# All loops written out, and matmuls without a reader, in a two-layer kernel of linear attention and patch-FFT convolution

## The reference

```python
x = x + L0(_gn(x), ...)   # attention without softmax, 6 heads of 64
x = x + L1(_gn(x), ...)   # 1x1 conv, filter in 8x8 patches, 3x3 depthwise conv, gate, 1x1 conv

# L0
q = elu(rope(Wq x + bq) * scale) + 1;  k = elu(rope(Wk x + bk)) + 1;  v = Wv x + bv
kv = einsum('bhnd,bhne->bhde', k, v)
normalizer = einsum('bhnd,bhd->bhn', q, k.sum(axis=2))[..., None]
out = einsum('bhnd,bhde->bhne', q, kv) / (normalizer + 1e-06)
return conv1x1(out, Wfc, bfc)

# L1
t = einsum('bchw,oc->bohw', x, w_in)
t = irfft2(rfft2(patches of 8x8 of t) * fft_filter)
t = depthwise 3x3 conv of t with w_dw, 'SAME'
g = gelu(t[:, :192]) * t[:, 192:]
return einsum('bchw,oc->bohw', g, w_out)
```

## Time and profile before

| | us |
|---|---|
| median of 3 runs | 3960.15 |
| lowest, highest | 3959.14, 3964.23 |
| the profiled execution | 3959.47 |
| its span | 3957.6 |
| its mean granted clock, of full | 0.944 |

### The profile page before, as it was taken

One profiled execution on the slowest core, in us unless ns is written; L12 is line 12 of the kernel. 1 busy time (PEld: TensorE's weight loads), 2 busy tenths in 40 slices (PEclk: granted clock), 3 DMA queues, 4 the chain that ended last, 5 costly groups with the idle time before them and its releaser, 6 DMA issues.

```text
span 3957.6 us, 61233 instructions
## 1 busy us (share of the span) xinstructions
PE 3490.4 (88%) x17808; PEld 3021.8 (76%) x17808; DVE 3178.0 (80%) x4879; ACT 1629.6 (41%) x2781; POOL 1795.7 (45%) x1114
## 2 busy tenths in 40 slices
PE   5988989889898898988989889897889979899798
PEld 4976779767796677966779677896768957699676
DVE  7976979769797697976879768897688976888777
ACT  2423634246342463425633255332553316533164
POOL 2543535435354353553435534454344544444443
PEclk9998989999998999999989899898999989999899
DMA  5113322133212332123321233213332133221322
GB/s 201 64 56 136 119 77 69 64 120 120 89 56 72 121 119 81 57 87 120 112 76 61 88 112 112 89 48 103 109 107 81 48 114 109 96 81 56 128 88 104
DMA packets 186274, 371.18 MB, mean 94 GB/s; under 512 B 7947, under 2 KB 9011, under 8 KB 185779
## 3 DMA queue, kind: packets, MB, share of 16 engines
q1 hardware_dynamic: 186034, 368.26, 27.2%
HBM read 267.56 MB, written 100.66 MB: 93 GB/s over the span
## 4 chain that ended last, share of the span: by engine, by line
issue 33%; PE 30%; POOL 18%; DVE 14%; ACT 3%; DMA 1%; POOLq 1%; DVEq 1%; SPq 0%; ACTq 0%
POOL t L445 9%; POOL x_lo L438 6%; PE bank L1234 5%; PE bank L1200 3%; DVE bank L942 3%; PE bank L1075 3%; PE bank L1076 3%; PE bank L1080 3%; POOL qn L482 3%; PE bank L1207 3%; DVE nrm L850 2%; DVE qt_lo L865 2%; PE bank L1154 2%; DVE xr L878 2%; DVE bn_x L911 2%
## 5 line engine op out<-in xcount | busy, mean ns | idle before, releaser
L445 POOL TENSOR_TENSOR t<-t 128x768 f32<-128x768 f32 x256 | 535.4, 2092 | 726.4 <-DVE t L786 726.4
L1076 PE MATMUL bank<-w_lo,x_hi 128*128 128x384 f32 x2322 | 792.7, 341 | 34.1 <-issue 34.1
L1075 PE MATMUL bank<-w_hi,x_hi 128*128 128x384 f32 x2322 | 789.7, 340 | 4.0 <-ACT x_hi L537 4.0
L438 POOL TENSOR_TENSOR x_lo<-xa,x_hi 128x512 fp32r<-128x512 f32 x363 | 495.9, 1382 | 592.0 <-ACT x_hi L537 592.0
L942 DVE SCALAR_TENSOR_TENSOR bank<-big,wdw,bank 128x512 f32<-128x512 f32 x960 | 685.7, 750 | 94.5 <-PE bank L1234 91.3
L506 POOL TENSOR_TENSOR prod<-prod 128x512 f32<-128x512 f32 x320 | 409.1, 1278 | 489.1 <-ACT prod L629 479.0
L542 ACT ACTIVATE t<-t 128x768 f32<-128x768 f32 x256 | 217.1, 848 | 929.1 <-POOL t L445 929.1
L1080 PE MATMUL bank<-w_hi,x_lo 128*128 128x384 f32 x2322 | 542.3, 342 | 0.5 <-POOL x_lo L438 0.5
L796 DVE SCALAR_TENSOR_TENSOR kt<-t 128x384 f32<-128x384 f32 x256 | 533.6, 2084 | 0.0
L1076 PEld LDWEIGHTS bank<-w_lo,x_hi 128*128 128x128 f32 x2322 | 441.4, 190 | 36.3 <-issue 36.3
L1075 PEld LDWEIGHTS bank<-w_hi,x_hi 128*128 128x128 f32 x2322 | 442.3, 190 | 5.1 <-ACT x_hi L537 4.4
(11 more groups left out here) (127 smaller groups left out, 6800.2 us busy)
## 6 DMA issues: line engine op xcount, KB each, us to landing
xr<-x SPq DMA_DIRECT2D x128, 768.0 KB, 4.7
xa<-x SPq DMA_DIRECT2D x66, 768.0 KB, 6.0
x_scratch<-xr SPq DMA_DIRECT2D x64, 768.0 KB, 3.5
xa<-x_scratch SPq DMA_DIRECT2D x64, 768.0 KB, 5.9
xr<-x_scratch SPq DMA_DIRECT2D x64, 768.0 KB, 4.8
out<-xr SPq DMA_DIRECT2D x64, 768.0 KB, 3.5
big<-x SPq DMA_DIRECT2D x8, 768.0 KB, 10.3
w_raw<-wqkv_t SPq DMA_DIRECT2D x1, 1728.0 KB, 7.3
```

Of the source, the lines that this page charges most:

```text
L438: nc.gpsimd.tensor_tensor(dst, src, hi, ALU.subtract).then_inc(s_lo, 1)
L445: nc.gpsimd.tensor_tensor(a, a, b[:, :, ::-1, :], ALU.add).then_inc(s_add, 1)
L1075: nc.tensor.matmul(dst, hi(k), whi(k), start=first and k == 0, stop=False)
L1076: nc.tensor.matmul(dst, hi(k), wlo(k), start=False, stop=False)
```

## The change

Every `Fori` becomes a Python loop: the one over images and those over chunks, on all five engines. And TensorE gets `keep_warm(n, free)`: n matmuls of 128x512 on weights that lie in SBUF, into a PSUM bank that is free there, whose result nobody reads. They stand in front of waits: 4 and 6 ahead of the last two `add_kv` of an image, 4 ahead of L1136, 2 ahead of L1139, 10 ahead of the first transposes, 14 ahead of the group norm, 6 between its two halves, 10 behind it, and 30 ahead of the last step's output blocks in part C: 86 for each image.

```diff
-        def steps(eng, total, lo, hi, body):
-
-            for c in range(lo):
-                body(c, c // 2, c, c % 2)
-            if lo >= hi:
-                return
-            with eng.Fori(0, (hi - lo) // 2) as k:
-                for u in range(2):
-                    body(k * 2 + (lo + u), k + (lo + u) // 2, None, (lo + u) % 2)
-            for c in range(hi, total):
+        def steps(total, body):
+
+            for c in range(total):
                 body(c, c // 2, c, c % 2)
...
-            with pe.Fori(0, images) as i:
+            for i in range(images):
...
+            def keep_warm(n, free):
+
+                for _ in range(n):
+                    nc.tensor.matmul(bank[free][:, :], win_hi[:, 0, 0:P], w_hi[:, 0, 0:CHUNK], start=True, stop=True)
+
+            def group_avg(f, n_warm=0, free=0):
 
                 for step, (wait, src) in enumerate(((1, lambda k: mv[:, :, k, 0]), (4, lambda k: dev[:, :, k]))):
+                    if step == 1:
+                        keep_warm(n_warm, free)
...
                         project(T + 4, m + 1, 1 - par, 0)
+                    if edge == NCH - 1:
+                        keep_warm(4, 5)
                     add_kv(T + 2, 2)
                     if within(edge, 0, NCH, 1):
                         project(T + 5, m + 1, 1 - par, 1)
+                    if edge == NCH - 1:
+                        keep_warm(6, 5)
                     add_kv(T + 3, 3, last=(edge == NCH - 1))
...
+                keep_warm(4, 5)
                 pe.wait_ge(s_kd, i * 5 + 2)
                 nc.tensor.matmul(bank[0][:, 0:C], ones_f[:, :], kdiag[:, :, :], start=True, stop=True).then_inc(s_kp, 1)
+                keep_warm(2, 5)
...
+                keep_warm(10, 5)
                 transpose_q(0, 0)
...
-                steps(pe, NCH, 0, NCH - 2, part_b)
-                group_avg(i + 1)
+                steps(NCH, part_b)
+                keep_warm(14, 0)
+                group_avg(i + 1, 6, 0)
+                keep_warm(10, 0)
...
+                    if last:
+                        keep_warm(30, 3)
                     if prod:
                         out_block(c - 2, 0, last)
```

More of the change, by code:

```diff
@@ L359, in wait @@
                 sp.sem_inc(s_past, 1)
-            with sp.Fori(0, images) as i:
+            for i in range(images):
                 def load_next(c, h, par):
@@ L374, in load_a @@
                     load_next(c + 2, h + 1, par)
-                steps(sp, NCH - 2, 0, NCH - 2, load_a)
+                steps(NCH - 2, load_a)
                 def part_b(c, h, edge, par):
@@ L387, in part_b @@
                         sp.dma_start(xr[:, par], chunk_of(x_v, i, c)).then_inc(s_xr[par], 16)
-                steps(sp, NCH + 2, 2, NCH, part_b)
+                steps(NCH + 2, part_b)
                 wait(s_x1s, i * 8 + (NCH + 2))
@@ L414, in part_c @@
                         sp.dma_start(xr[:, par], chunk_of(x1_v, i, c)).then_inc(s_xr[par], 16)
-                steps(sp, NCH + 2, 2, NCH - 2, part_c)
+                steps(NCH + 2, part_c)
             for par in range(2):
@@ L448, in _ @@
                 low_part(0, k, 0)
-            with gp.Fori(0, images) as i:
+            for i in range(images):
                 rotated_sum(i * NT, 0)
@@ L459, in part_a @@
                             rotated_sum(T + j + 1, (j + 1) % 2)
-                steps(gp, NCH, 0, NCH - 2, part_a)
+                steps(NCH, part_a)
                 gp.wait_ge(s_ka, i * 5 + 1)
@@ L487, in part_b @@
                         times_ksum(c + 1, 1 - par)
-                steps(gp, NCH, 0, NCH - 2, part_b)
+                steps(NCH, part_b)
                 gp.wait_ge(s_qn, i * NCH + (NCH + 1))
@@ L514, in part_c @@
                             low_part(i * 16 + c + (NCH + 1), k, 1 - par, patches=(edge != NCH - 1))
-                steps(gp, NCH + 1, 1, NCH - 1, part_c)
+                steps(NCH + 1, part_c)
         @block.scalar
@@ L555, in _ @@
             high_part(0, 0)
-            with act.Fori(0, images) as i:
+            for i in range(images):
                 tile_a(i * NT, 0)
@@ L566, in part_a @@
                             tile_a(T + j + 1, (j + 1) % 2)
-                steps(act, NCH, 0, NCH - 2, part_a)
+                steps(NCH, part_a)
                 act.wait_ge(s_kp, i * 5 + 1)
@@ L585, in part_b @@
                         nc.scalar.activation(qt_hi[:, par, j], bank[(par + j) % 2][:, :], ACT.Copy).then_inc(s_qt, 1)
-                steps(act, NCH, 0, NCH, part_b)
+                steps(NCH, part_b)
                 group_root(i + 1)
@@ L673, in part_c @@
                         copy_img(T + 3, c, 3)
-                steps(act, NCH + 2, NCH + 2, NCH + 2, part_c)
+                steps(NCH + 2, part_c)
         @block.vector
@@ L802, in _ @@
             rope(0, 0, 0)
-            with dve.Fori(0, images) as i:
+            for i in range(images):
                 def part_a(c, h, edge, par):
@@ L821, in part_a @@
                         elu(T + j, c * 4 + j, j % 2)
-                steps(dve, NCH, 0, NCH - 2, part_a)
+                steps(NCH, part_a)
                 kvp = bank[KVB][:, 0:KB * (P + 1)].rearrange("p (k n) -> p k n", k=KB)
@@ L915, in part_b @@
                         low_q(c + 1, 1 - par, (2,))
-                steps(dve, NCH + 1, 1, NCH - 1, part_b)
+                steps(NCH + 1, part_b)
                 group_norm(i + 1)
@@ L1045, in part_c @@
                         add_out(2, 2, last)
-                steps(dve, NCH + 2, 4, NCH - 2, part_c)
+                steps(NCH + 2, part_c)
         @block.tensor
@@ L1054, in _ @@
             nc.tensor.matmul(bank[6][:, 0:C], sel, fsel[:, :], start=True, stop=True).then_inc(s_filter, 1)
-            def group_avg(f):
+            def keep_warm(n, free):
+                for _ in range(n):
+                    nc.tensor.matmul(bank[free][:, :], win_hi[:, 0, 0:P], w_hi[:, 0, 0:CHUNK], start=True, stop=True)
+            def group_avg(f, n_warm=0, free=0):
                 for step, (wait, src) in enumerate(((1, lambda k: mv[:, :, k, 0]), (4, lambda k: dev[:, :, k]))):
+                    if step == 1:
+                        keep_warm(n_warm, free)
                     pe.wait_ge(s_gs, f * 11 + wait)
@@ L1129, in part_a @@
                         project(T + 5, m + 1, 1 - par, 1)
+                    if edge == NCH - 1:
+                        keep_warm(6, 5)
                     add_kv(T + 3, 3, last=(edge == NCH - 1))
-                steps(pe, NCH, 2, NCH - 2, part_a)
+                steps(NCH, part_a)
+                keep_warm(4, 5)
                 pe.wait_ge(s_kd, i * 5 + 2)
                 nc.tensor.matmul(bank[0][:, 0:C], ones_f[:, :], kdiag[:, :, :], start=True, stop=True).then_inc(s_kp, 1)
+                keep_warm(2, 5)
                 pe.wait_ge(s_kd, i * 5 + 4)
@@ L1279, in part_c @@
                         project((i + 1) * NT + 1, (i + 1) * 16, 0, 1)
-                steps(pe, NCH + 2, 2, NCH, part_c)
+                steps(NCH + 2, part_c)
 def kernel(x, L0_conv_Wq, L0_conv_bq, L0_conv_Wk, L0_conv_bk, L0_conv_Wv, L0_conv_bv, L0_conv_Wfc, L0_conv_bfc,
```

## The result

The changed kernel takes 3824.98 us (median of 4 runs, 3821.55 to 3832.74) beside 3959.64 us for the kernel before (4 runs on the same chip, 3957.45 to 3964.23): a ratio of 0.966 (95% interval 0.964 to 0.968), 135 us less. The profiled execution took 3824.6 us. One execution each of two kernels further down ran in a slower state (3995 and 6086 us) and is left out of their medians.

What follows compares the result with a forecast made beforehand. It took the span to be decided where TensorE stands still or runs at half clock: 3959.5 - 66 (jumps) - 12 (end of C) - 10 (end of A, kv) - 12 (group norm) = 3859 us; range 3833 to 3895.

Steps and rivals of the forecast that it cites:

- The jump: Entry into each later image: writing out the image loop removes TensorE's stops and half clock, 9.4 us each, seven times, 66 us.
- The inner loops: Chunk loops on all five engines: writing them out gains nothing, since looped and written-out chunks have equal pitch.
- The waits against registers become waits against constants: Waits in the written-out code: nothing gained, since project(1) with constants and project(2) with registers both take 5.10 us.
- The group norm: Between parts B and C: 14, 6 and 10 fillers gain 1.5 us an image, ends -2 and 3; 12 us in all.
- End of C: Wait ahead of the last output blocks: 30 fillers gain 1.6 us each time, ends 0 and 2.7; 12 us in all.
- end of A with the kv step: Gaps up to part B's first transposes: 4 + 6 + 4 + 2 + 10 fillers gain 1.3 us an image; 10 us in all.
- A: Rival at all filled places: fillers give nothing, as the clock falls anyway or overlong ones cost; 3893 us, chance 0.12.
- B: Rival at the image jump: the long stop is slow code fetch in traffic, in straight code too; 3900 us, chance 0.05.
- C: Rival throughout: straight code stalls on instruction fetch, 4.9 us a stop; 4055 us with five per image, chance 0.03.
- D: Rival at all filled places: everything holds and the clock never falls there, upper ends; 3833 us, chance 0.12.

Runs made afterwards that it cites:

- the second run: The 86 matmuls without a reader for each image added to the kernel before, all loops kept: 3909.81 us, ratio 0.988.
- the kernel without the thirty fillers: The changed kernel without the 14, 6 and 10 fillers of each group norm: 3842.48 us, ratio 0.971 to the kernel before.
- the first register try: The changed kernel with part B of TensorE, POOL and VectorE in single-trip loops, which were folded into constants: 3830.11 us, ratio 0.967 to the kernel before.
- the kernel with seventeen: The changed kernel with seventeen instead of ten fillers ahead of part B's first transposes: 3837.79 us, ratio 0.968 to the kernel before.

## Why the prediction was wrong, and where it was right

- **The jump: right.** 9.4 us for each of seven, 66 in all, was read from image 1 against image 3. Measured: 20.01 to 10.20, 69 in all; the entry takes 10.20 us with the image loops alone as with TensorE's alone. What was late next was as argued: nothing.
- **"The inner loops ... nothing, by the equal pitch of looped and written-out chunks", "The waits against registers become waits against constants ... so nothing again": the failed step.** The rows that carried it, 5.77 us for a tile of part A and 5.10 twice for project, are from stretches in which PE is busy throughout (and from chunks written out; the looped ones of part A have 5.77 too). There a register instruction can hide behind matmuls, and part A indeed stayed at 172.3 us without any. Part B's length is a ring of waits over four engines, with PE idle in each turn, and its pitch was never compared. A comparison of its looped and straight chunks would have misled as well: both have 9.90, since the straight ones still compute their waits from the image's number. The row to see was the hand-over itself: the stop of 1.04 us ahead of the transposes that ends with POOL's product, of which 0.25 us lie behind the product's end, and a register instruction stands ahead of that wait. In its place the runs showed 0.25 us for each chunk, 0.14 at the wait of TensorE and 0.14 ahead of VectorE's product, less some hundredths elsewhere, and 18 us in all from the loops (84.97 to 82.73), 16 of them by 64 times 0.25; the rest of part B's 21 is where the clock falls. So the loops won 92 us by themselves and not 66.
- **The group norm: mechanism right, term mis-sized.** It stood at 12 us (1.5 an image, ends -2 and 3) and is 24.5 with the start of C, the upper end. L1063 takes 1.72 and 1.62 us at full clock, not 1.9; the clock held in seven images of eight; and some 6 us of it are the loops' (9.92 + 181.85 with the loops alone against 10.04 + 182.50), which may be computed waits or addresses taken away, or jumps in part C; that wasn't tried.
- **End of C, and end of A with the kv step: right.** 13 and 10 us against 12 and 10, of which the loops alone bring 3 at the end of C (5.44 to 5.06 us). The clock held at both in all eight images.
- **Start: not in the sum.** -2.4 us, which other runs show to vary.
- **The rivals.** A (fillers give nothing, 3893) falls by the second run, 49 us. B (the long stop isn't the jump's, 3900) falls by TensorE's loops alone. C (straight code stalls) falls: more instructions are fetched, 150 packets on the larger queue against 118 (3.26 MB on both instruction queues against 2.92), and PE has no long stop for "issue" at an image's start. The Trainium skill, "Runtime: NRT & Kernel Launch", section on instruction fetch mechanics, says that refills of sequential code are mostly hidden; this kernel agrees. D (3833) was the nearest, and even it left out part B. The range's lower end was built on the fillers alone; a term costed at nothing had no end of its own there, and that is why the time fell out of it.

## What to carry to other kernels

Before a term is costed at nothing, ask whether the stretch it was read from has the same bound as the stretch it is meant for: a register instruction cost nothing here where its engine was busy, and 0.14 us where the engine had waited for a hand-over of the ring that sets the pace. Split "the loop" into the jump and the computed waits and addresses, since they are paid at different places. Filler matmuls are worth timing site by site: more of them in one stage can move the fall of the clock into the next.

## What the hardware showed that was not expected

- A wait whose value is computed in a register made a hand-over 0.14 us longer on PE (0.24 against 0.10 from POOL's end to the transposes, medians), with no loop around it.
- Two products that VectorE and POOL begin within 0.24 us of each other hold each other up: as a rule VectorE's takes 0.96 us and POOL's 2.04 to 2.29, ending 1.33 behind VectorE's, and in 14 chunks of one kernel, where both began within 0.01 us, VectorE's took 2.28 and POOL's 1.47. So a later start of VectorE's product delays the end of POOL's.
- Of the five engines' jumps back to the next image only TensorE's cost time: 9.8 us each, with the time at half clock behind it.
- Fourteen L1063 in a row (3.15 us, PE listed busy) don't bring the clock up (in the kernel without the thirty fillers), but with fillers ahead of them it stayed up through both groups in seven of eight images (1.72 and 1.62 us), and without the six in between in four.
- The falls differ between programs that hardly differ: read in windows of 0.5 us, the changed kernel's clock falls 10 times, and that of the first register try, with 51200 instructions against 51128 and the same work, 15 times; within the first two chunks of part B in five images and in all eight. The second is 5 us slower. The Trainium skill, "TensorE: Matmul & The Clock Gate", Part 1, says that the number of slow matmuls varies from run to run of one kernel. The runs here agree: five executions of the kernel with seventeen have a mean granted clock of 0.987 to 0.994 and take 3842 to 3826 us. So a difference of 5 us between two kernels here can't be put down to one edit.
